# P V of an attention block in 64x64 tiles by blocks of 64 keys, in two stages over two PSUM banks

## The chip, the cores and the metric

One core of one Trainium2 chip. The metric is the device time of one execution in microseconds. TensorE is PE in the profile (its weight loads PEld), VectorE DVE, ScalarE ACT, GpSimd POOL, SyncE SP.

## The reference

Eight sequences of 256 tokens, model width 128. Each is normalised and goes through causal attention with 16 heads of 64 and, beside it, through a feed-forward block with ternary weights (width 512); both are added to the input.

```python
xn = _layernorm(x, axis=-1)
# attention, on a second normalisation of xn with weight ln_w and bias ln_b
q, k, v = (einsum('bsd,hde->bshe', x2, W) + bias for each)
scores  = einsum('bqhe,bkhe->bhqk', q, k) * 64 ** -0.5     # -inf where key > query
pattern = softmax(scores, axis=-1)
z       = einsum('bhqk,bkhe->bqhe', pattern, v)             # the "P V" of the title
attn    = einsum('bqhe,hed->bqd', z, W_o) + b_o
h       = relu(einsum('bsd,fd->bsf', xn, ternary(W1)) + b1)
ffn     = einsum('bsf,df->bsd', h, ternary(W2)) + b2
out     = x + attn + ffn
```

## The kernel before

The host lays each sequence out "by place": tokens 0 to 127, then 192 to 255, then 128 to 191. So places 128 to 191 hold the last 64 tokens. A "pair" is two heads (8 pairs), a "duo" is two pairs (4 duos). Batch is one sequence.

For each batch the steps are: normalisation (POOL, with statistics on DVE); its transposes xh and xn on PE; eight projections pr0 to pr7 (queries and keys of one pair, three f32r passes of high and low parts) with a copy to qk on ACT (L474, L476); four value products v0 to v3 (half of the heads by half of the tokens) with a copy to v on DVE (L622); scores s0 to s7 per pair, plain f32 in 64x64 tiles of PE (L816): row half by head, column half by query block; per head maxima m on DVE (L597) and exponentials e on ACT (L485, L487); reciprocals i on DVE; division p on POOL (L308, L309); a 32x32-block transpose t on DVE per pair (L610); then d, four transfers per duo issued by SP (L345) that bring the blocks into pT; then z, the product of v and the turned probabilities per duo (`heads`, L834 to L860); its high part zT_hi on ACT (L497) and its low part zT_lo on DVE (L616); f0, f1 and h0, h1, the feed-forward; and the output product in two parts, oa and ob, closed on DVE by o and stored by SP (st).

In `heads`, per pair and head, the keys of token tile 0 (128 partitions, all rows of PE) are multiplied for all 256 queries, and the keys of tile 1 for the 128 later queries only; the two heads of a pair stand in the two column halves of PE. So there are 8 matmuls per duo, in f32, and each matmul is two records in the profile. All of them go into one PSUM bank of 512 f32: pair 0 in its first half, pair 1 in its second.

The order of work on every engine is written out by hand in strings: a head (batches 0 and 1), a plan that is repeated for batches 2 to 6, and a tail (batch 7). Each engine works through its own string in order. In a string, `s3` is scores of pair 3, `z1-` is heads of duo 1 of the batch before, `pr0+` a projection of the next batch. On PE the number behind the colon is the PSUM bank (of four in m_ps) into which the step writes; before it writes, `wait_taken` (L732) waits until the step that had this bank before was read out. Scores have banks of their own (s_ps, two pairs by two heads), so scores of pair n wait for the exponentials of pair n - 2 (L811). For the bank of heads the step that sets it free is zT_lo on DVE.

In the last batch the last two pairs are not turned by DVE and transfers but by PE (tw, tn), since nothing is left to hide the transfers.

## Time and profile before

| | us |
|---|---|
| median of 3 runs | 227.62 (227.01 to 228.51) |
| profiled execution | 227.57 |
| its span, first to last instruction | 225.8 |
| PE busy in the span | 216.5 (96%) |
| DVE busy | 201.5 (89%) |
| ACT busy | 195.4 (87%) |
| POOL busy | 184.8 (82%) |

The granted clock was 1.00 in all stretches, that is 2.4 GHz. The span is smaller than the device time by what lies around the first and the last instruction. In the timeline and in the chain a row gives start and length; matmuls overlap, so what a block costs PE is the distance from its start to the next block's start and not its length. A fused row ("x40") stands for so many records of the same line.

### The profile page before, as it was taken

The numbers are of one execution on the slowest core, as the hardware profiler recorded it, in microseconds if no ns is written. First come the engines' busy times: TensorE is split into PE (matmuls) and PEld (weight loads), VectorE is DVE, ScalarE is ACT, GpSimd is POOL, SyncE is SP. The second block draws the span as 40 slices with busy tenths as digits, with TensorE's granted clock in tenths as the row PEclk, the third lists the DMA queues.
The fourth block names the chain that finished last, engine by engine and source line by source line (L and its number), as shares of the span: only waits on it lengthen the run. The fifth ranks groups of instructions, "written<-read, shape, count | busy, mean of one in ns | idle before, by whom it ended". The sixth has DMA issues, their size and how long they took to land.

```text
span 225.8 us, 7611 instructions
## 1 busy us (share of the span) xinstructions
PE 216.5 (96%) x2646; PEld 182.9 (81%) x2646; DVE 201.5 (89%) x776; ACT 195.4 (87%) x733; POOL 184.8 (82%) x363
## 2 busy tenths in 40 slices
...
GB/s 155 300 247 3 116 167 141 140 66 126 142 139 142 119 117 137 154 104 149 165 142 142 104 131 133 144 103 142 172 127 169 73 137 134 180 105 192 207 41 23
DMA packets 24022, 30.66 MB, mean 136 GB/s; under 512 B 2608, under 2 KB 23088, under 8 KB 23984
## 3 DMA queue, kind: packets, MB, share of 16 engines
...
q14 instruction: 17, 0.14, 0.2%
...
## 4 chain that ended last, share of the span: by engine, by line
PE 41%; POOL 20%; ACT 15%; DVE 12%; DMA 6%; issue 2%; SPq 2%; POOLq 0%; DVEq 0%
PE s_ps L816 8%; PE m_ps L854 7%; POOL prob L309 5%; ACT prob L485 5%; DMA pT<-blocks 4%; POOL prob L308 4%; ACT prob L487 4%; DVE s_ps L597 4%; PE m_ps L781 4%; DVE blocks L610 4%; POOL xn_cur L388 3%; PE m_ps L858 3%; PE m_ps L782 3%; PE m_ps L783 3%; ACT qk L474 2%
## 5 line engine op out<-in xcount | busy, mean ns | idle before, releaser
L485 ACT ACTIVATE prob<-s_ps,neg_max 128x256 f32<-128x256 f32 x128 | 69.3, 541 | 10.5 <-DVE neg_max L597 10.3
L597 DVE CUSTOM_DVE_ANT_0 s_ps<-s_ps,causal 128x256 f32<-128x256 f32 x128 | 54.7, 427 | 8.3 <-PE s_ps L816 8.1
L309 POOL TENSOR_SCALAR prob<-prob,inv_sum 128x256 f32<-128x256 f32 x126 | 61.6, 489 | 0.0
L610 DVE STREAM_TRANSPOSE blocks<-prob 128x768 f32<-128x768 f32 x62 | 58.8, 962 | 0.8 <-POOL prob L309 0.3
L308 POOL TENSOR_SCALAR prob<-prob,inv_sum 128x128 f32<-128x128 f32 x126 | 48.1, 382 | 13.4 <-DVE inv_sum L604 13.3
L487 ACT ACTIVATE prob<-s_ps,neg_max 128x128 f32<-128x128 f32 x128 | 55.4, 433 | 0.0
L816 PE MATMUL s_ps<-qk 64*64 64x64 f32 (+2 forms) x1280 | 46.7, 278 | 0.8 <-ACT prob L487 0.7
L816 PEld LDWEIGHTS s_ps<-qk 64*64 64x64 f32 x1280 | 39.1, 132 | 9.7 <-issue 4.7
L854 PE MATMUL m_ps<-pT,v 128*64 128x256 f32 x256 | 40.0, 388 | 2.5 <-DMA pT<-blocks 2.5
L597 DVE CUSTOM_DVE_ANT_0 s_ps<-s_ps,causal_first 128x128 f32<-128x128 f32 x128 | 42.3, 331 | 0.0
L474 ACT ACTIVATE qk<-m_ps,vecs 128x256 f32<-128x256 f32 x64 | 34.9, 546 | 2.0 <-PE m_ps L783 1.6
L597 DVE DVE_READ_ACCUMULATOR2_ANT neg_max<- 128x1 f32 x256 | 36.1, 141 | 0.0
L476 ACT ACTIVATE qk<-m_ps,vecs 128x256 f32<-128x256 f32 x64 | 35.3, 553 | 0.0
L487 ACT ACTIVATION_READ_ACCUMULATOR prob<-s_ps,neg_max 128x1 f32 x128 | 34.6, 270 | 0.0
L485 ACT ACTIVATION_READ_ACCUMULATOR prob<-s_ps,neg_max 128x1 f32 x128 | 33.7, 263 | 0.0
L858 PEld LDWEIGHTS m_ps<-pT,v 128*64 128x64 f32 x256 | 19.1, 137 | 8.5
L858 PE MATMUL m_ps<-pT,v 128*64 128x128 f32 x256 | 25.2, 273 | 0.0
L616 DVE TENSOR_TENSOR zT_lo<-m_ps,zT_hi 128x512 fp32r<-128x512 f32 x32 | 21.9, 686 | 2.7 <-ACT zT_hi L497 2.4
L497 ACT ACTIVATE zT_hi<-m_ps 128x512 fp32r<-128x512 f32 x32 | 20.7, 647 | 3.6 <-PE m_ps L858 3.5
L622 DVE COPY v<-m_ps 128x512 f32<-128x512 f32 x32 | 21.6, 678 | 0.3 <-PE m_ps L804 0.3
L439 POOL TENSOR_TENSOR hT_lo<-hT,hT_hi 128x512 fp32r<-128x512 f32 x16 | 20.7, 1291 | 1.3
L854 PEld LDWEIGHTS m_ps<-pT,v 128*64 128x64 f32 x256 | 15.1, 136 | 5.4 <-issue 3.3
...
## 6 DMA issues: line engine op xcount, KB each, us to landing
...
```

Of the source, the lines that this page charges most:

```text
L308: op(first, first, inv_sum[:, j, 2 + h:3 + h], 0.0, ALU.mult, ALU.add)
L309: last = op(later, later, inv_sum[:, j, h:h + 1], 0.0, ALU.mult, ALU.add)
L474: nc.scalar.activation(qk[:, j, 0, :], halves("pr", pair, b)[:, 0, :], ACT.Identity, bias=vecs[:, BQ + pair:BQ + pair + 1])
L476: last = nc.scalar.activation(qk[:, j, 1, :].rearrange("e (g j k) -> e g j k", g=TILES, j=QT), halves("pr", pair, b)[:, 1, :].rearrange("e ...
L485: nc.scalar.activation(later, s_ps[:, pair % 2, h, 0:S].rearrange("p (g j k) -> p g j k", g=TILES, j=QT), ACT.Exp, bias=neg_max[:, j, h:h ...
L487: nc.scalar.activation(first, s_ps[:, pair % 2, h, S:W].rearrange("p (j k) -> p j k", j=QT), ACT.Exp, bias=neg_max[:, j, 2 + h:3 + h], sca ...
L597: last = nc.vector.tensor_tensor_reduce(out=sc, in0=sc, in1=mask, scale=-SCALE, scalar=-MASKED, op0=ALU.add, op1=ALU.min, accum_out=neg_ma ...
L610: nc.vector.transpose(blocks[:, duo, :, n, :, :], prob[:, pair % NBUF, :, :, :, :] .rearrange("p h j g k -> p (j g) h k")).then_inc(turned, 1)
L616: nc.vector.tensor_tensor(zT_lo[:, both, :], halves("z", duo, b), zT_hi[:, both, :].bitcast(F32), ALU.subtract).then_inc(z_lo, 1)
L816: return nc.tensor.matmul(at[side * E:side * E + E], qk[rows, j, 0, places], keys[rows], start=True, stop=True)
L854: nc.tensor.matmul(dst[h * E:h * E + E, n, :], v[:, 0, cols], turned_parts(n, h)[0], start=True, stop=False)
L858: last = nc.tensor.matmul(dst[h * E:h * E + E, n, P:S], v[:, 1, cols], turned_parts(n, h)[1], start=False, stop=True)
```

## The change

Heads are worked in 64x64 tiles. The keys of a token tile are split into two blocks of 64, one in each row half of PE, and every product is cut to the queries that may see the block: keys 0 to 63 by all 256 queries, keys 64 to 127 by 192 of them, keys 128 to 191 by 128, keys 192 to 255 by 64. `heads(b, duo, stage)` has two stages. In stage 0 (step y) the first row half works on the duo's pair 0 and the later row half on pair 1, in stage 1 (step z) the row halves work on the other pair. Pair 0 is accumulated in one PSUM bank and pair 1 in another, so that a step x (which issues nothing) and the step y each name a bank; the two row halves never write into one bank within a stage. Stage 1 waits for stage 0 by a new semaphore, heads_half. Stage 0 has 5 products, stage 1 has 7, each for two heads: 24 matmuls per duo instead of 8. The copies of heads on ACT and DVE read 256 columns from each of two banks instead of 512 of one.

The orders of all engines are new, also in the head and the tail. In the steady plan y and z of duos 0 to 3 of the batch before now stand among the first part of the batch, with a block of scores between y and z of each duo.

The diff, cut; head and tail strings are left out here but for PE's tail and the first line of ACT's head, the two of the new text that stand between.

```diff
--- before
+++ after
...
-PE_PLAN = ("z1-:2 s1 pr4:3 v0:0 pr5:2 v1:1 pr6:3 s2 s3 oa-:2 f0:3 z2-:1 z3-:0 s4 s5 pr7:1 v2:3 ob- v3:3 xh+:0 "
-           "f1:2 s6 s7 z0:0 pr0+:1 pr1+:2 pr2+:3 pr3+:1 xn+:0 s0+")
...
-ACT_PLAN = ("pr7- e9- e10- e11- xh f1- e12- e13- z0- pr0 e14- pr1 e15- xn pr2 e0 z1- e1 pr3 pr4 e2 e3 pr5 pr6 e4 "
-            "e5 e6 e7 z2- z3- f0 e8")
...
-DVE_PLAN = ("m1 xn z1- m2 t7- m3 v0 ln+ i0 i1 m4 v1 m5 t0 i2 m6 m7 t1 t2 z2- m8 z3- m9 m10 i3 v2 m11 o- i4 t3 xh+ "
-            "m12 m13 v3 m14 i5 i6 m15 z0 t4 t5 m0+ i7 t6")
...
-POOL_PLAN = ("p0 p1 p2 ln+ p3 xl+ p4 p5 p6 p7 h0 h1")
...
-SP_PLAN = ("d1- d2- d3- d0 st-")
...
+PE_PLAN = ("s0 x0-:1 y0-:2 s1 z0- pr4:0 pr5:3 x1-:1 y1-:2 s2 z1- v0:0 pr6:3 x2-:2 y2-:1 s3 z2- s4 pr7:3 v1:0 "
+           "x3-:2 y3-:1 s5 z3- s6 v2:3 v3:0 xh+:2 oa-:1 f0:0 f1:2 s7 pr0+:0 xn+:3 pr1+:2 ob- pr2+:0 pr3+:3")
+PE_TAIL = ("s0 x0-:0 y0-:1 s1 pr4:2 z0- x1-:3 s2 y1-:2 z1- x2-:0 y2-:1 s3 z2- pr5:2 v0:3 s4 pr6:2 v1:3 pr7:0 "
+           "x3-:2 y3-:1 s5 z3- s6 oa-:3 ob- x0:0 y0:1 s7 z0 v2:2 f0:3 x1:0 y1:1 z1 tw6:2 v3:3 x2:1 tw7:0 tn3:2 "
+           "f1:3 y2:0 z2 x3:3 y3:2 z3 oa:1 ob oc")
+ACT_HEAD = ("wh0 wh1 pr0 wh2 xn pr1 wh3 e0 e1 pr2 aa e2 pr3 e3 pr4 pr5 e4 e5 pr6 pr7 f0 e6 e7 xh+ e8 e9 xn+ f1 "
...
+ACT_PLAN = ("e13- e14- pr0 xn e15- pr1 pr2 pr3 e0 z0- e1 e2 pr4 pr5 z1- e3 e4 e5 pr6 z2- e6 e7 e8 e9 pr7 z3- e10 "
+            "xh+ e11 e12 f0 f1")
...
+DVE_PLAN = ("ln+ m2 z0- m3 i0 t7- m4 m5 z1- t0 i1 v0 m6 m7 z2- m8 m9 t1 i2 v1 m10 m11 i3 z3- v2 m12 i4 v3 xh+ t2 "
+            "t3 i5 m13 m14 m15 i6 t4 t5 xn+ t6 o- i7 m0+ m1+")
...
+POOL_PLAN = ("p1 ln+ p2 p3 xl+ p4 p5 p6 h0 p7 p0+ h1")
...
+SP_PLAN = ("d3- d0 d1 d2 st-")
...
+        def heads_banks(duo, b):
+
+            low, high = sorted((BANK["x", duo, b], BANK["y", duo, b]))
+            return m_ps[:, low:high + 1:high - low, 0:S]
...
-                wait(sp, z_psd, DUOS * (b - 1) + duo + 1)
+                wait(sp, z_psd, 4 * (DUOS * (b - 1) + duo + 1))
...
-                wait(act, z_psd, PAIRS // 2 * b + duo + 1)
-                nc.scalar.activation(zT_hi[:, 2 * duo:2 * duo + 2, :], halves("z", duo, b), ACT.Copy).then_inc(z_hi, 1)
+                wait(act, z_psd, 4 * (DUOS * b + duo + 1))
+                nc.scalar.activation(zT_hi[:, 2 * duo:2 * duo + 2, :], heads_banks(duo, b), ACT.Copy).then_inc(z_hi, 1)
...
-                nc.vector.tensor_tensor(zT_lo[:, both, :], halves("z", duo, b), zT_hi[:, both, :].bitcast(F32),
+                nc.vector.tensor_tensor(zT_lo[:, both, :], heads_banks(duo, b), zT_hi[:, both, :].bitcast(F32),
...
-                elif kind == "z":
+                elif kind in "xy":
...
-            def heads(b, duo):
-                if duo % 2 == 0:
-                    wait(pe, v_done, 4 * b + duo + 2)
+            def heads(b, duo, stage):
                 by_tensor = on_tensor_engine(b, 2 * duo)
-                if by_tensor:
-                    pe.wait_ge(last_wide, 2)
-                    pe.wait_ge(last_narrow, 1)
+                dst = heads_banks(duo, b)
+                first, later = slice(0, E), slice(E, P)
+                whole, lower, upper, near, far, both = (slice(0, QT), slice(0, 2), slice(2, QT), slice(0, 1), slice(1, 2),
+                                                        slice(0, 2))
+                def product(n, rows, tile, queries, i, done=None, closes=False):
+                    clears = tile == 0 and rows == (first if n == 0 else later) and queries.start == 0
+                    toks = slice(queries.start * P + i.start * QB, (queries.stop - 1) * P + i.stop * QB)
+                    for h in range(2):
+                        cols = slice((2 * (2 * duo + n) + h) * E, (2 * (2 * duo + n) + h) * E + E)
+                        if by_tensor:
+                            turned_part = pT_last[rows, n, h, tile * P + toks.start:tile * P + toks.stop]
+                        else:
+                            turned_part = pT[rows, duo, i, tile + queries.start:tile + queries.stop, n, h, :]\
+                                .rearrange("p i g q -> p g i q")
+                        last = nc.tensor.matmul(dst[h * E:h * E + E, n, toks], v[rows, tile, cols], turned_part,
+                                                start=clears, stop=closes)
+                        if done is not None:
+                            last.then_inc(done, 1)
+                if stage == 0:
+                    if duo % 2 == 0:
+                        wait(pe, v_done, 4 * b + duo + 2)
+                    if by_tensor:
+                        pe.wait_ge(last_wide, 2)
+                        pe.wait_ge(last_narrow, 1)
+                    else:
+                        pe.wait_ge(pT_in[duo], 16 * QT * (b + 1))
+                    product(0, first, 0, both, whole)
+                    product(1, later, 0, near, upper)
+                    product(1, later, 0, far, whole)
+                    product(1, later, 1, far, whole, heads_half)
+                    product(0, first, 1, far, lower, heads_half)
                 else:
-                    pe.wait_ge(pT_in[duo], 16 * QT * (b + 1))
-                dst = halves("z", duo, b)
-
-                def turned_parts(n, h):
-                    if by_tensor:
-                        return pT_last[:, n, h, 0:S], pT_last[:, n, h, S:W]
-                    return pT[:, duo, :, 0:2, n, h, :].rearrange("p i g q -> p g i q"), pT[:, duo, :, 2, n, h, :]
-
-                for n in range(2):
-                    pair = 2 * duo + n
-                    for h in range(2):
-                        cols = slice((2 * pair + h) * E, (2 * pair + h) * E + E)
-                        nc.tensor.matmul(dst[h * E:h * E + E, n, :], v[:, 0, cols], turned_parts(n, h)[0],
-                                         start=True, stop=False)
-                    for h in range(2):
-                        cols = slice((2 * pair + h) * E, (2 * pair + h) * E + E)
-                        last = nc.tensor.matmul(dst[h * E:h * E + E, n, P:S], v[:, 1, cols], turned_parts(n, h)[1],
-                                                start=False, stop=True)
-                last.then_inc(z_psd, 1)
+                    wait(pe, heads_half, 4 * (DUOS * b + duo + 1))
+                    product(0, later, 0, near, upper)
+                    product(1, first, 0, near, lower)
+                    product(0, later, 0, far, whole)
+                    product(1, first, 0, near, upper)
+                    product(1, first, 0, far, whole)
+                    product(0, later, 1, far, whole, z_psd, closes=True)
+                    product(1, first, 1, far, lower, z_psd, closes=True)
...
+                elif kind == "x":
+                    pass
+                elif kind == "y":
+                    heads(b, index, 0)
                 elif kind == "z":
-                    heads(b, index)
+                    heads(b, index, 1)
```

## Rows read from the trace of the kernel before

**Rows 1.** The page, part 1: busy time, share of span, and instructions of each engine.

```profile
PE 216.5 (96%) x2646; PEld 182.9 (81%) x2646; DVE 201.5 (89%) x776; ACT 195.4 (87%) x733; POOL 184.8 (82%) x363
```

**Rows 2.** Stretches: from and to, length, busy time of each engine, clock, DMA share, GB/s.

```profile
12.00:39.00 27.00, 25.66 (x293) 19.96 (x295) 25.22 (x107) 26.72 (x105) 25.38 (x46) 1.00 0.54 130
...
64.60:89.80 25.20, 25.20 (x332) 21.93 (x328) 23.89 (x93) 23.00 (x91) 20.42 (x43) 1.00 0.60 133
89.80:115.60 25.80, 25.57 (x334) 22.09 (x328) 24.69 (x99) 23.63 (x92) 22.36 (x46) 1.00 0.60 137
115.60:141.90 26.30, 25.32 (x334) 22.11 (x329) 24.70 (x96) 23.80 (x92) 22.85 (x46) 1.00 0.60 135
141.90:167.20 25.30, 25.30 (x333) 22.01 (x329) 23.92 (x93) 23.10 (x90) 21.01 (x42) 1.00 0.55 132
...
190.40:210.00 19.60, 19.31 (x258) 15.98 (x253) 18.66 (x75) 18.63 (x74) 16.78 (x35) 1.00 0.71 158
```

**Rows 3.** Waits from 64 to 167 us: waiter, releaser, us in total, times, longest.

```profile
PE m_ps L854 <- DMA pT<-blocks: 1.2, 2, 1.0
...
DVE s_ps L597 <- PE s_ps L816: 3.5, 11, 0.6
...
ACT prob L485 <- DVE neg_max L597: 7.0, 14, 0.9
```

**Rows 4.** Timeline of PE, 98 to 104 us: start, length, line, operation.

```profile
98.08 0.65 PE L854 MATMUL m_ps<-pT,v 128*64 128x256 f32 x4
...
100.52 0.39 PE L858 MATMUL m_ps<-pT,v 128*64 128x128 f32 x4
100.84 1.34 PE L816 MATMUL s_ps<-qk 64*64 64x256 f32 x40
102.10 0.38 PE L781 MATMUL m_ps<-x2T_hi,wq_lo 128*128 128x256 f32 x1
...
102.92 0.40 PE L802 MATMUL m_ps<-wv_hi,x2T_lo 128*128 128x512 f32 x1
...
103.62 0.28 PE L924 MATMUL m_ps<-zT_hi,wo_lo 128*128 128x256 f32 x1
```

**Rows 5.** Timeline of PE, 113 to 116 us.

```profile
113.45 0.65 PE L854 MATMUL m_ps<-pT,v 128*64 128x256 f32 x4 [0.22 <-DMA pT<-blocks]
...
114.90 0.78 PE L816 MATMUL s_ps<-qk 64*64 64x256 f32 x20
115.61 0.39 PE L781 MATMUL m_ps<-x2T_hi,wq_lo 128*128 128x256 f32 x1
```

**Rows 6.** Chain that ended last, 131 to 140 us: start, length, what.

```profile
131.59 0.99 DVE blocks L610
132.60 0.55 SPq L345
...
134.58 5.00 DMA pT<-blocks
...
139.72 0.65 PE m_ps L854 x4
```

**Rows 7.** Groups by line, shapes apart: busy us and mean ns, then idle before.

```profile
L616 DVE TENSOR_TENSOR zT_lo<-m_ps,zT_hi 128x512 fp32r<-128x512 f32 x32 | 21.9, 686 | 2.7 <-ACT zT_hi L497 2.4
...
L497 ACT ACTIVATE zT_hi<-m_ps 128x512 fp32r<-128x512 f32 x32 | 20.7, 647 | 3.6 <-PE m_ps L858 3.5
```

**Rows 8.** Timeline of ACT, 88 to 90 us.

```profile
88.10 0.56 ACT L474 ACTIVATE qk<-m_ps,vecs 128x256 f32<-128x256 f32 x1
...
88.82 0.58 ACT L485 ACTIVATE prob<-s_ps,neg_max 128x256 f32<-128x256 f32 x1
...
89.61 0.72 ACT L497 ACTIVATE zT_hi<-m_ps 128x512 fp32r<-128x512 f32 x1
90.11 0.59 ACT L485 ACTIVATE prob<-s_ps,neg_max 128x256 f32<-128x256 f32 x1
```

**Rows 9.** Timeline of DVE, 91 to 93 us.

```profile
90.97 0.42 DVE L597 CUSTOM_DVE_ANT_0 s_ps<-s_ps,causal 128x256 f32<-128x256 f32 x1
...
91.56 0.97 DVE L610 STREAM_TRANSPOSE blocks<-prob 128x768 f32<-128x768 f32 x1
92.45 0.40 DVE L597 CUSTOM_DVE_ANT_0 s_ps<-s_ps,causal 128x256 f32<-128x256 f32 x1
```

More of the change, by code:

```diff
@@ L48 @@
 BUSY = (5, 1)
-PE_HEAD = ("xb:0 pr0:0 pr1:3 xn:2 s0 s1 v0:3 pr2:1 pr3:2 v1:3 s2 v2:1 s3 pr4:3 ta:0 pr5:2 pr6:1 s4 pr7:3 v3:0 "
-           "xh+:1 f0:2 s5 s6 pr0+:0 bo:2 f1:1 pr1+:3 s7 xn+:0 z0:1 s0+ pr2+:3 pr3+:2 pr4+:0 s1+ pr5+:1 z1:3 s2+ "
-           "z2:2 s3+ pr6+:0 oa:3 f0+:1 s4+ z3:0 s5+ v0+:1 v1+:2 pr7+:0 ob v2+:1 v3+:2 xh++:3 f1+:0 s6+ s7+ z0+:1 "
-           "pr0++:0 pr1++:2 pr2++:3 xn++:0 pr3++:1 s0++")
-PE_PLAN = ("z1-:2 s1 pr4:3 v0:0 pr5:2 v1:1 pr6:3 s2 s3 oa-:2 f0:3 z2-:1 z3-:0 s4 s5 pr7:1 v2:3 ob- v3:3 xh+:0 "
-           "f1:2 s6 s7 z0:0 pr0+:1 pr1+:2 pr2+:3 pr3+:1 xn+:0 s0+")
@@ L55 @@
-PE_TAIL = ("pr4:2 s1 z1-:3 v0:0 s2 pr5:1 pr6:0 s3 z2-:2 s4 pr7:3 s5 z3-:1 oa-:0 f0:3 s6 s7 f1:1 v1:3 v2:2 v3:1 "
-           "ob- z0:3 z1:2 tw6:1 tn3:0 tw7:3 z2:1 z3:0 oa:2 ob oc")
-ACT_HEAD = ("wh0 wh1 pr0 pr1 wh2 wh3 xn e0 e1 pr2 e2 e3 pr3 aa e4 e5 pr4 e6 e7 pr5 pr6 e8 xh+ e9 f0 pr7 e10 e11 "
-            "pr0+ e12 f1 e13 pr1+ e14 z0 xn+ e15 pr2+ oh e0+ e1+ pr3+ e2+ e3+ pr4+ z1 wh4 e4+ pr5+ e5+ e6+ pr6+ "
-            "z2 e7+ f0+ wh5 z3 e8+")
-ACT_PLAN = ("pr7- e9- e10- e11- xh f1- e12- e13- z0- pr0 e14- pr1 e15- xn pr2 e0 z1- e1 pr3 pr4 e2 e3 pr5 pr6 e4 "
-            "e5 e6 e7 z2- z3- f0 e8")
@@ L62 @@
-ACT_TAIL = ("pr7- e9- e10- e11- xh f1- e12- e13- z0- pr0 e14- pr1 e15- pr2 xn e0 pr3 e1 z1- pr4 e2 e3 e4 e5 pr5 "
-            "e6 e7 pr6 pr7 e8 z2- e9 z3- e10 e11 f0 f1 e12 e13 e14 e15 z0 w6 w7 z1 z2 z3")
-DVE_HEAD = ("lz nh xb wl0 wl1 m0 m1 xn v0 m2 i0 m3 ln+ v1 i1 t0 m4 m5 m6 v2 th i2 m7 te0 m8 m9 i3 t1 v3 xh+ m10 "
[3 rows of a table removed]
-DVE_PLAN = ("m1 xn z1- m2 t7- m3 v0 ln+ i0 i1 m4 v1 m5 t0 i2 m6 m7 t1 t2 z2- m8 z3- m9 m10 i3 v2 m11 o- i4 t3 xh+ "
-            "m12 m13 v3 m14 i5 i6 m15 z0 t4 t5 m0+ i7 t6")
-DVE_TAIL = ("m1 xn m2 t7- m3 i0 v0 m4 m5 z1- m6 i1 m7 i2 t0 m8 t1 m9 i3 m10 t2 m11 i4 t3 z2- i5 z3- t4 m12 t5 m13 "
-            "m14 v1 i6 m15 v2 v3 i7 o- q7 z0 n3 z1 z2 z3 o")
@@ L72 @@
-POOL_HEAD = ("hs np wl2 wl3 p0 ln+ p1 p2 p3 xl+ p4 h0 p5 h1 p6 p7 ol p0+ p1+ wl4 ln++ wl5 p2+ p3+ h0+ xl++ p4+ p5+ "
-             "p6+ p7+ h1+")
-POOL_PLAN = ("p0 p1 p2 ln+ p3 xl+ p4 p5 p6 p7 h0 h1")
-POOL_TAIL = ("p0 p1 p2 p3 p4 p5 h0 h1 p6")
-SP_HEAD = ("d0 d1 d2 d3 d0+ st")
-SP_PLAN = ("d1- d2- d3- d0 st-")
-SP_TAIL = ("d1- d2- d3- d0 d1 d2 st- st")
+PE_HEAD = ("xb:2 pr0:0 pr1:3 xn:2 s0 v0:1 pr2:3 s1 v1:1 pr3:3 s2 pr4:1 ta:0 pr5:2 s3 pr6:3 f0:0 pr7:2 s4 v2:3 "
[3 rows of a table added]
+PE_PLAN = ("s0 x0-:1 y0-:2 s1 z0- pr4:0 pr5:3 x1-:1 y1-:2 s2 z1- v0:0 pr6:3 x2-:2 y2-:1 s3 z2- s4 pr7:3 v1:0 "
+           "x3-:2 y3-:1 s5 z3- s6 v2:3 v3:0 xh+:2 oa-:1 f0:0 f1:2 s7 pr0+:0 xn+:3 pr1+:2 ob- pr2+:0 pr3+:3")
```

13 lines of the change are left out of this document (added), and 9 rows, old and new, of tables (DVE_HEAD, PE_HEAD).

## The prediction, made before the change was run

> **What bounds the kernel now.** I read the busy shares first: PE, DVE, ACT and POOL lie between 216.5 and 184.8 us of a 225.8 us span [rows 1], so the share alone does not name the bound. The table of stretches does. Its cuts are where the fifth pair of projections of batches 2, 3, 4, 5 and 6 begins: four batches in 25.2, 25.8, 26.3 and 25.3 us, mean 25.65, with PE busy all the time in two of them, and DVE on average (23.89 + 24.69 + 24.70 + 23.92) / 4 = 24.3 us, ACT 23.4, POOL 21.7 [rows 2]. The waits of the same stretch say it again: PE waited 1.2 us in 103, for two late loads of pT; DVE waited 3.5 us for PE's scores, and ACT 7.0 us for DVE's maxima [rows 3]. So in the steady part PE's order sets the time, 0.3 us per batch is lost to transfers, and DVE is the next bound, only 1.3 us per batch below. In the first part (12 to 39 us) ACT is busy 26.72 of 27.00 us, and in 190 to 210 us ACT 18.63 of 19.60 [rows 2]: there a shorter PE gives little.
>
> **PE, the part that is removed.** Start to start, four heads halves in a row (two duos of 16 records) run from 98.08 to 100.84: 1.38 us a duo; one alone between scores runs from 113.45 to 114.90: 1.45 us [rows 4, 5]. The old steady plan has z2 z3 together and z1 and z0 alone: 2.76 + 2 x 1.45 = 5.66 us per batch. Scores: alone 0.71 us (114.90 to 115.61), two in a run 1.26 (100.84 to 102.10), so one more block in an unbroken run of 64x64 tiles costs 0.55 and each run pays 0.16 for entering and leaving [rows 4, 5]. Old scores: two alone, three runs of two: 2 x 0.71 + 3 x 1.26 = 5.20. Together 10.86 us.
>
> **PE, the part that is added.** A pair of heads streams 256 + 128 columns through all rows. In blocks of 64 keys a row half streams 256 + 64 for one pair, and 64 + 128 + 128 for the other, so 320 columns in each stage, the two halves side by side, the two heads in the column halves. That is what a scores block does: per column half 256 + 64 and 128 + 64 + 128, ten products, twenty records, and two banks. The first stage also has ten products. I therefore price it at 0.55. The second stage has fourteen products for the same 320 columns; no row shows it. Below: 0.55, as its columns are the same. Above: 0.71, a block that pays for a run of its own [rows 5]. I take 0.60, since it is nearest to the scores block. The new plan has five runs of 64x64 work per batch (s0 y0 s1 z0; y1 s2 z1; y2 s3 z2 s4; y3 s5 z3 s6; s7), 16 blocks: 5 x 0.71 + 11 x 0.55 + 4 x 0.05 = 9.80 us. PE gains 10.86 - 9.80 = 1.06 per batch, 1.26 with the lower bound and 0.62 with the upper. The wait of the second stage for the first costs nothing in this plan: a block of scores (0.55) lies between. Where y and z stand side by side (two places in the head, three in the tail) the drain is on PE; below 0, above 0.39, the length of the last records of a heads block [rows 4]. These at most 2.0 us lie mostly where ACT leads, and at the very end the cheaper blocks pay them back (two duos 2.76 before, 4 x 0.58 + 2 x 0.2 = 2.7 after), so I book nothing.
>
> By the Trainium skill (TensorE: Matmul & The Clock Gate, Part 3, the mechanism of packing) matmuls start and end strictly in program order, also across tiles. Then a tile would stand still while another works off its turn. Counted through for a scores block, with two passes to a product and each pass begun only after the one before has begun, that is 448 column times where the tiles side by side need 320. The trace disagrees: at 0.55 / 320 = 1.72 ns a column the rule would give 0.77 us, and a further block takes 0.55 [rows 4, 5].
>
> **ACT, DVE and POOL** do the same work. The copy of the heads (647 ns) and its low part (686 ns) [rows 7] now read 256 columns from each of two banks instead of 512 from one; same count of elements, so nothing is added. Eight semaphore increments per duo instead of one are sent by matmuls that are there anyway. I cost both at 0 and at most 0.1 per duo, on the chain only where the next paragraph says.
>
> **What becomes late.** PE without waits would need 25.65 - 0.3 - 1.06 = 24.3 us, the same as DVE's busy time. So PE can gain 1.35 per batch at the very most, and new waits take from it. I went through a batch from s0 at 0 with durations of rows: scores of 0.55, a projection after scores 0.82 (102.10 to 102.92), values 0.70 (102.92 to 103.62) [rows 4], maxima 0.59 a head, a turn 0.89 [rows 9], exponentials 0.79, a pair of projections on ACT 0.72, heads 0.50 [rows 8].
> First, banks. The old plan gave the heads one of four banks, the new one gives them two (1 and 2), from y to the end of the low part. z0 ends near 2.2, is in PSUM near 2.45; 0.65 on ACT and 0.69 on DVE behind what stands ahead of them give 4.0. PE wants y1 after pr4 and pr5 at 3.95. z1 is in PSUM at 5.95; ACT has pr4 and pr5 ahead until 6.05, then 0.65 and 0.69: 7.45; PE wants y2 at 7.4. So both are met with about 0.1 us each, no more.
> Second, transfers. t7 of the batch before stands on DVE behind statistics, a maximum, z0, a maximum: it ends near 5.4. In the trace a turn that ended at 132.58 let its heads start at 139.72: issue of four transfers on SP, then 5.00 us for the last one, 7.1 us in all [rows 6]. PE wants y3 (after y2 s3 z2 s4 pr7 v1) at 11.4; the data is there at 5.4 + 7.1 = 12.5 at the latest. The other pT wait of the trace was 0.2 long, so the way is often shorter; with 6.4 it is 11.8. The wait is 0.4 to 1.1; behind it in PE's queue stand s5, z3, s6, and DVE and ACT wait for those scores. In the old plan z3 came after oa and f0, at 98.08 + 1.38 = 99.46, 6.9 behind the end of t7 at 92.53 [rows 4, 9]. I take 0.5. s6 also needs the exponentials e8 and e9, which ACT ends near 13.5, about when PE comes there, so this wait is covered by the one before it.
> Sum: 24.3 + 0.1 (banks) + 0.5 (pT) = 24.9, 0.75 less than 25.65. The steady part is 39 to 190 us, six batches; the first and last have ACT's load near them, so I count five and a bit: 5.3 x 0.75 = 4.0 us. The profiled execution took 227.57 us, 0.05 below the median of 227.62, so both give **223.6 us**.
>
> **Rivals.**
> A, waits come to nothing: y3 finds its data, the banks turn in time. DVE bounds, 24.4: 5.3 x 1.25 = 6.6, **221 us**. For it: ACT and DVE still have 2.2 and 1.3 us of slack per batch [rows 2]. Against: 7.1 us from turn to heads is a measured row.
> B, the saving is eaten: y3 waits its full 1.1 (24.3 + 0.1 + 1.1 = 25.5, 0.15 x 5.3 = 0.8 us less), or the second stage costs 0.71 (0.44 more per batch) and the wait is 0.7: about **227 us**. For it: DVE and PE would both be full, with two score buffers between them, so that a wait of one is soon a wait of the other.
> C, slower: the transfer of the last duo sets the period. It is a loop: t7, 7.1 us, y3, s5, maxima, and on to the next t7. If t7 ends later than 5.4, because DVE waits there for ACT's copy of z0, each 0.1 us goes onto the batch. The gain is gone when that wait is 25.65 - 24.3 - 0.1 = 1.25, with 7.1 us of way that is t7's end at 11.4 + 1.25 - 7.1 = 5.55; it costs more than 1% (2.3 / 5.3 = 0.43 a batch) from 6.0 on. With t7 at 6.2 the wait is 1.9 and the batch 26.3: 0.65 x 5.3 = 3.4, **231 us**. Against it: 7.1 is the longest case of the trace, not the usual one.
> D, the row halves don't run side by side, so that products go in turn (the rule named above): the first stage is 448 column times, 0.77, the second 384, 0.66, together 1.43 a duo, nothing gained over 1.38 to 1.45 but fewer changes of tile, and the new waits stay: 25.65 - 0.3 + 0.1 + 0.5 = 25.95, **229 us**. Against it: [rows 4, 5], where four tiles of scores do run side by side.
>
> **Chances.** Forecast (222.3 to 225.2) 0.43; A 0.15; B 0.26; C 0.12; D 0.04. The predicted time is the forecast's. The range goes from 220.0, A's lower part, to 229.5, which leaves out most of C. A difference under about 1% can't be told from none here. Faster by over 1% (below 225.3): forecast and A, 0.58. Within 1%: B and half of D, 0.28. Slower: C and the other half, 0.14.
>
> **What would show it.** Steady batches of about 24.9 us instead of 25.65; blocks of the first stage 0.55 and of the second 0.55 to 0.71 apart in a run; DVE busy about 24.3 per batch, as before; a wait of PE for pT of 0.5 once per batch ahead of y3, with pT the first name in PE's waits; small waits of PE for DVE's zT_lo. ACT's waits for DVE's maxima should shrink. The prediction falls if the second stage is above 0.71, if DVE's or ACT's heads instructions grow by reading two banks, or if PE's waits exceed 1.4 us per batch.

## The result

The changed kernel takes 226.56 us (median of 20 runs, 225.15 to 228.59), the kernel before 227.8 us (20 runs, 227.01 to 229.64): ratio 0.9926, 95% interval 0.9902 to 0.9949. The ratio compares means, 226.41 against 228.10, and leaves out one slow run of the changed kernel (228.59). It is 0.7% faster, where 1.8% was forecast; the range held, the sign was right, the size was not. The profiled execution took 226.65 us, 0.92 less than that of before.

The page of the changed kernel, part 1, and its stretches, cut again where the fifth pair of projections of a batch begins (from 62.60 on: batches 2 to 6):

```profile
PE 212.5 (95%) x3670; PEld 187.4 (83%) x3670; DVE 202.1 (90%) x776; ACT 195.7 (87%) x733; POOL 182.5 (81%) x363
```

```profile
62.60:87.60 25.00, 24.41 (x461) 22.55 (x456) 24.27 (x97) 23.27 (x91) 22.85 (x45) 1.00 0.64 145
87.60:113.30 25.70, 24.80 (x463) 22.66 (x457) 24.66 (x97) 23.55 (x92) 21.93 (x44) 1.00 0.59 134
113.30:138.30 25.00, 24.19 (x460) 22.33 (x456) 24.39 (x96) 23.39 (x92) 21.86 (x44) 1.00 0.61 140
138.30:163.30 25.00, 24.66 (x463) 22.68 (x457) 24.37 (x97) 23.34 (x92) 21.84 (x44) 1.00 0.60 140
```

Against [rows 1] PE has 1,024 records more and 4 us less busy time. DVE, ACT and POOL have the same number of instructions and the same load within 1.3%. Against [rows 2] a batch is shorter, but PE is no longer busy all the time in any of them. The waits from 64 to 167 us, PE first, then its weight loads:

```profile
PE m_ps L863 <- DMA pT<-blocks: 1.9, 3, 0.8
PE s_ps L823 <- ACT prob L494: 0.2, 1, 0.2
```

```profile
PEld m_ps L863 <- issue: 3.7, 5, 1.2
PEld m_ps L863 <- DVE zT_lo L623: 1.7, 7, 0.3
```

The wait for pT (1.9 against 1.2 in [rows 3]) is larger and stands ahead of one step, y3. The wait for zT_lo is new: it is the PSUM banks of the heads. "Issue" stands on the same line, ahead of weight loads of the heads.

PE's timeline for most of a batch, from s0 to v2 (starts of blocks are what counts):

```profile
110.90 0.78 PE L823 MATMUL s_ps<-qk 64*64 64x256 f32 x20
111.50 0.74 PE L863 MATMUL m_ps<-pT,v 64*64 64x256 f32 x20
112.05 0.75 PE L823 MATMUL s_ps<-qk 64*64 64x256 f32 x20
112.60 0.75 PE L863 MATMUL m_ps<-pT,v 64*64 64x64 f32 x28
113.28 0.38 PE L788 MATMUL m_ps<-x2T_hi,wq_lo 128*128 128x256 f32 x1
...
115.04 0.78 PE L863 MATMUL m_ps<-pT,v 64*64 64x256 f32 x20
...
118.51 0.79 PE L863 MATMUL m_ps<-pT,v 64*64 64x256 f32 x20
119.08 0.77 PE L823 MATMUL s_ps<-qk 64*64 64x256 f32 x20
119.62 0.78 PE L863 MATMUL m_ps<-pT,v 64*64 64x64 f32 x28
120.24 0.78 PE L823 MATMUL s_ps<-qk 64*64 64x256 f32 x20
120.96 0.38 PE L788 MATMUL m_ps<-x2T_hi,wq_lo 128*128 128x256 f32 x1
121.76 0.39 PE L809 MATMUL m_ps<-wv_hi,x2T_lo 128*128 128x512 f32 x1
...
123.31 0.78 PE L863 MATMUL m_ps<-pT,v 64*64 64x256 f32 x20 [0.70 <-DMA pT<-blocks]
123.88 0.77 PE L823 MATMUL s_ps<-qk 64*64 64x256 f32 x20
124.43 0.78 PE L863 MATMUL m_ps<-pT,v 64*64 64x64 f32 x28
125.00 0.76 PE L823 MATMUL s_ps<-qk 64*64 64x256 f32 x20
125.69 0.50 PE L809 MATMUL m_ps<-wv_hi,x2T_lo 128*128 128x512 f32 x1
```

Stage 0 takes 0.55 to 0.57 (111.50 to 112.05, 118.51 to 119.08), stage 1 takes 0.57 to 0.62 ahead of scores (124.43 to 125.00, 119.62 to 120.24) and 0.68 ahead of a projection (112.60 to 113.28). From s0 at 110.90, y1 starts at +4.14, y2 at +7.61, y3 at +12.41; the walk of the prediction had 4.0, 7.5 and 11.8 to 12.5. Values v1 at 121.76 should let y3 start 0.8 later; it starts 1.55 later.

### The profile page after: what moved, and what is told of

Same layout as the page of the kernel before. It is cut to its first block, busy times and chain, and to the rows that moved or that the text cites. A ratio compares the mean times of both kernels' runs of the same rounds, so it can differ in the third digit from the quotient of the medians.

```text
span 224.9 us, 9676 instructions
## 1 busy us (share of the span) xinstructions
PE 212.5 (95%) x3670; PEld 187.4 (83%) x3670; DVE 202.1 (90%) x776; ACT 195.7 (87%) x733; POOL 182.5 (81%) x363
## 3 DMA queue, kind: packets, MB, share of 16 engines
HBM read 4.73 MB, written 1.05 MB: 26 GB/s over the span
## 4 chain that ended last, share of the span: by engine, by line
PE 38%; DVE 23%; DMA 11%; ACT 10%; POOL 8%; SPq 4%; issue 3%; POOLq 0%; DVEq 0%
DMA pT<-blocks 11%; DVE s_ps L604 9%; PE m_ps L863 6%; PE s_ps L823 6%; DVE blocks L617 6%; SPq L352 4%; ACT prob L492 3%; PE m_ps L941 3%; ACT prob L494 2%; PE m_ps L788 2%; PE s_ps L734 2%; DVE neg_max L604 2%; PE m_ps L790 2%; PE m_ps L789 2%; DVE zT_lo L623 2%
## 5 line engine op out<-in xcount | busy, mean ns | idle before, releaser
L492 ACT ACTIVATE prob<-s_ps,neg_max 128x256 f32<-128x256 f32 x128 | 65.4, 511 | 2.6 <-DVE neg_max L604 2.3
L863 PE MATMUL m_ps<-pT,v 64*64 64x64 f32 (+2 forms) x1536 | 50.0, 257 | 5.9 <-DMA pT<-blocks 3.5
L863 PEld LDWEIGHTS m_ps<-pT,v 64*64 64x64 f32 x1536 | 42.8, 133 | 12.1 <-issue 5.8
L494 ACT ACTIVATE prob<-s_ps,neg_max 128x128 f32<-128x128 f32 x128 | 51.7, 404 | 0.0
L823 PE MATMUL s_ps<-qk 64*64 64x128 f32 (+2 forms) x1280 | 49.7, 275 | 0.8 <-ACT prob L494 0.6
L823 PEld LDWEIGHTS s_ps<-qk 64*64 64x64 f32 x1280 | 42.1, 133 | 5.6 <-issue 3.3
L481 ACT ACTIVATE qk<-m_ps,vecs 128x256 f32<-128x256 f32 x64 | 33.8, 528 | 1.1 <-PE m_ps L784 0.8
L483 ACT ACTIVATE qk<-m_ps,vecs 128x256 f32<-128x256 f32 x64 | 34.3, 536 | 0.0
L494 ACT ACTIVATION_READ_ACCUMULATOR prob<-s_ps,neg_max 128x1 f32 x128 | 31.0, 242 | 0.0
L492 ACT ACTIVATION_READ_ACCUMULATOR prob<-s_ps,neg_max 128x1 f32 x128 | 30.2, 236 | 0.0
L788 PE MATMUL m_ps<-x2T_hi,wq_lo 128*128 128x256 f32 x56 | 18.7, 333 | 0.8 <-issue 0.6
L510 ACT ACTIVATE hT<-m_ps,vecs 128x256 f32<-128x256 f32 x32 | 12.8, 478 | 3.4 <-PE m_ps L930 3.4
```

The source lines that it names most:

```text
L481: nc.scalar.activation(qk[:, j, 0, :], halves("pr", pair, b)[:, 0, :], ACT.Identity, bias=vecs[:, BQ + pair:BQ + pair + 1])
L483: last = nc.scalar.activation(qk[:, j, 1, :].rearrange("e (g j k) -> e g j k", g=TILES, j=QT), halves("pr", pair, b)[:, 1, :].rearrange("e ...
L492: nc.scalar.activation(later, s_ps[:, pair % 2, h, 0:S].rearrange("p (g j k) -> p g j k", g=TILES, j=QT), ACT.Exp, bias=neg_max[:, j, h:h ...
L494: nc.scalar.activation(first, s_ps[:, pair % 2, h, S:W].rearrange("p (j k) -> p j k", j=QT), ACT.Exp, bias=neg_max[:, j, 2 + h:3 + h], sca ...
L788: nc.tensor.matmul(dst, wlo[kind][:, cols], x2T_hi[:, :], start=True, stop=False)
L823: return nc.tensor.matmul(at[side * E:side * E + E], qk[rows, j, 0, places], keys[rows], start=True, stop=True)
```

## Where the time of a steady batch went

The distance from each PE block's start to the next one's, for the five batches between s0 of batch 2 and s0 of batch 7, splits a batch. The least distance that a block shows in any batch of the kernel and of its variants with equal blocks (three executions of the kernel before, seven of the changed one) is taken as its cost without a wait; what is above it is counted as waiting. The split leans on this choice: with each kernel's own execution alone the waits are 0.73 and 1.10, and the blocks save 0.86. The length of a batch comes from one profiled execution of each kernel; differences of a tenth between two runs mean little.

| us per batch | before | changed | difference | predicted |
|---|---|---|---|---|
| s0 to s0 of the next batch, mean of five | 25.73 | 25.24 | -0.48 | -0.75 |
| sum of the blocks without waits | 24.88 | 23.83 | -1.05 | -1.06 |
| waits | 0.84 | 1.41 | +0.57 | +0.3 |

In the kernel before, 0.39 of the waits stand ahead of z1; the rest is in pieces below 0.08. In the changed kernel they are ahead of y3 (0.68), of y1 (0.18, banks), and after z1 and z3 (0.10 each); the rest is in pieces below 0.06.

The saving of the blocks hides two errors that cancel: the sixteen blocks of heads and scores went from 10.88 to 9.61 (forecast: 10.86 to 9.80), but the other blocks went from 14.00 to 14.21. The new order has five runs of heads and scores a batch instead of four, and a projection or values block behind a 64x64 run or ahead of one takes 0.77 to 0.80 from start to start, where one between two of its like takes 0.68 to 0.69. Of this the prediction had only what the scores blocks show.

From s0 of batch 2 to s0 of batch 7 the changed kernel wins 2.4 us (before: 61.10 to 189.72; changed: 60.22 to 186.43). At s0 of batch 2 it is 0.88 ahead, but has still to do a duo of heads (y0 and z0, 1.23 us) that the old order had behind it: like for like it is 0.35 late. From s0 of batch 7 to the end it takes 2.4 us longer, of which 1.23 are that duo: 1.1 to 1.2 us are lost in the tail. 2.4 - 0.35 - 1.15 = 0.9, the difference of the two spans.

## The experiments

Ratios are to runs of the kernel before on the same chip, with their 95% intervals; they can differ by up to 0.2% from the quotient of the two medians. The changed kernel's own is 0.993 (0.990 to 0.995).

**1. Old products in the new order.** What do the tiles give, what does the order?

```diff
             def heads(b, duo, stage):
+                if stage == 0:
+                    return
...
+                        nc.tensor.matmul(dst[h * E:h * E + E, n, :], v[:, 0, cols], turned_parts(n, h)[0],
+                                         start=True, stop=False)
...
+                last.then_inc(z_psd, 4)
```

> The new orders, banks and copies, but the old heads: step y issues nothing, step z issues the eight matmuls over all rows, each pair into its own bank. Theory (the products save PE about 1.1 us per batch in this order; the new waits for banks and pT eat half of it, the tail the rest): steady batches grow from 25.2 to 25.9-26.4 us, the total to 230-233 us, ratio to before 1.01 to 1.025. Rival (the orders carry the 0.7% gain, the tiles nothing): the total stays at 226-227 us.

Measured: 231.39 us, ratio 1.0153 (1.0123 to 1.0183). The orders carry nothing by themselves: with the old products they cost 1.5%, and the tiles turn that into a gain of 0.7%, 2.3% between the two. A steady batch takes 25.99 us (61.17 to 191.14 for five) against 25.24 and 25.73. In 64 to 167 us PE has no wait of 0.2 us or more for pT: with dearer heads PE reaches z3 after its transfer has landed. So the products save 0.75 a batch in this order. The five batches of this run agree block by block within 0.02 us, and their blocks add up to 25.98 against 23.83: the products take up to 2.15 off PE's blocks here (less by whatever wait stands alike in every batch of this run), and most of it comes back as waits. What the new products would do in the old order was not run.

**2. The wait ahead of y3 taken away.** The heads of duo 3 read duo 2's part of pT.

```diff
-                        pe.wait_ge(pT_in[duo], 16 * QT * (b + 1))
+                        pe.wait_ge(pT_in[2 if duo == 3 else duo], 16 * QT * (b + 1))
...
-                            turned_part = pT[rows, duo, i,
+                            turned_part = pT[rows, 2 if duo == 3 else duo, i,
```

> The changed kernel, but in batches 0 to 6 the heads of duo 3 read the turned probabilities of duo 2, whose transfers have landed long before (all transfers are still made; wrong values for duo 3's heads). It takes away the wait ahead of y3 alone. Theory (this wait costs 0.5 us a batch and is on PE's path): PE's waits for pT in 64 to 167 us fall from 1.9 to near 0, steady batches 24.7 us, total 224-225 us. Rival (DVE or the banks would hold PE at the same place anyway): steady batches stay at 25.1-25.2, total within 0.5 us of the changed kernel.

Measured: 224.81 us, ratio 0.9865 (0.9838 to 0.9893); a steady batch is 25.02. The wait of 0.68 is gone, but only 0.22 of it is won. PE's timeline around y3 in this run:

```profile
120.98 0.39 PE L809 MATMUL m_ps<-wv_hi,x2T_lo 128*128 128x512 f32 x1
...
121.77 0.78 PE L863 MATMUL m_ps<-pT,v 64*64 64x256 f32 x20
122.36 0.74 PE L823 MATMUL s_ps<-qk 64*64 64x256 f32 x20
122.91 0.81 PE L863 MATMUL m_ps<-pT,v 64*64 64x64 f32 x28
123.92 0.78 PE L823 MATMUL s_ps<-qk 64*64 64x256 f32 x20 [0.20 <-ACT prob L494]
```

y3 comes 0.79 after v1, without a wait. But from z3 to s6 it is now 1.01 instead of 0.57 (124.43 to 125.00 above): s6 waits for the exponentials of pair 4. That wait was named in the prediction as "covered by the one before it". Over the five batches 0.26 of the 0.68 stand there now, 0.15 between y3 and s5 (in one batch), and 0.11 around z1.

**3. The banks released early.** ACT and DVE read a quarter of each heads bank, release it, and spend the other three quarters on SBUF.

```diff
-                nc.scalar.activation(zT_hi[:, 2 * duo:2 * duo + 2, :], heads_banks(duo, b), ACT.Copy).then_inc(z_hi, 1)
+                nc.scalar.activation(zT_hi[:, 2 * duo:2 * duo + 2, 0:E], heads_banks(duo, b)[:, :, 0:E], ACT.Copy).then_inc(z_hi, 1)
+                nc.scalar.activation(zT_hi[:, 2 * duo:2 * duo + 2, E:S],
+                                     wo[:, 0:3, :].rearrange("p a d -> p (a d)").rearrange("p (n s) -> p n s", n=2), ACT.Copy).then_inc(z_rest, 1)
...
+                nc.vector.tensor_tensor(zT_lo[:, both, 0:E], heads_banks(duo, b)[:, :, 0:E], zT_hi[:, both, 0:E].bitcast(F32),
+                                        ALU.subtract).then_inc(z_free, 1)
+                still = wo[:, 0:3, :].rearrange("p a d -> p (a d)").rearrange("p (n s) -> p n s", n=2)
+                nc.vector.tensor_tensor(zT_lo[:, both, E:S], still, still, ALU.subtract).then_inc(z_lo, 1)
```

> The changed kernel, but the two PSUM banks of a duo come free after a quarter of the heads copies: ACT and DVE read 64 of 256 columns of each bank, then release it, and spend the rest of the time on 384 columns read from SBUF (three quarters of the heads values are replaced, so the output is another). Turn-round of a bank shrinks by about 0.8 us, the load of ACT and DVE grows by about 0.1 to 0.3 us a duo for the second instruction. Theory (waiting for banks costs 0.4 us a batch): PE's waits for zT_lo go to 0, steady batches 24.8-25.0 us, total 224-226 us. Rival (DVE bounds the steady part): steady batches longer, 25.3 or more, by the added DVE time.

Measured: 230.53 us, ratio 1.0113 (1.007 to 1.0155). Both halves of the expectation came: no wait of PE for zT_lo is left in 64 to 167 us, and the batches got longer, 25.52. The stretch 65 to 165 us, first of the changed kernel, then of this one:

```profile
65.00:165.00 100.00, 97.41 (x1813) 89.54 (x1802) 96.99 (x376) 92.85 (x358) 87.52 (x176) 1.00 0.61 140
```

```profile
65.00:165.00 100.00, 97.39 (x1760) 88.75 (x1762) 97.39 (x385) 93.06 (x371) 88.72 (x173) 1.00 0.60 137
```

The added instructions cost DVE 4.7 us over the run (206.8 busy against 202.1) and ACT 2.8; POOL is busy 6.9 us longer with no instruction of its own added. The span grows by 3.8 us: 1.6 up to s0 of batch 2, 1.4 in five steady batches, 0.8 behind them. What the banks alone cost is not told by it, nor which of the three engines costs the time.

**4. DVE relieved, in both kernels.** Each copy of values moves half of its columns from batch 1 on.

```diff
-                nc.vector.tensor_copy(v[:, t, HALF[half]], bank("v", n, b)).then_inc(v_done, 1)
+                copied = H * E // 4 if b else H * E // 2
+                nc.vector.tensor_copy(v[:, t, half * H * E // 2:half * H * E // 2 + copied], bank("v", n, b)[:, 0:copied]).then_inc(v_done, 1)
```

> The changed kernel with DVE relieved: from the second batch on each of the four copies of values moves 256 of 512 columns (the other half of v keeps the first batch's values), about 0.27 us less each, 1.1 us of DVE per batch. Theory (after the change PE is still the first bound, with waits for pT and banks, and DVE second): steady batches 25.2 to 24.9 us, total 0.5 to 1.5 us less than the changed kernel. Rival (DVE bounds the steady part now): batches 24.2 to 24.4 us, total 4 to 5 us less, 222 us.

> The same relief of DVE in the kernel before. Theory (PE sets the time there, waiting 1.2 us in 103): steady batches fall by 0.2 us or less from 25.7, total by up to 1 us. Rival (DVE is already part of the bound): total 3 us less or more.

Measured: changed kernel 225.48 us, 0.9907 (0.987 to 0.9945); before 227.42 us, 0.9996 (0.9958 to 1.0034). Steady batches 25.17 and 25.68, each 0.05 to 0.07 less for 0.8 us less DVE work (23.7 instead of 24.5 busy in a batch; the expectation had 1.1). The sum of DVE's work bounds neither, and the rival falls; the theory's 24.9 did not come either. The copies of values lie outside the stretch of DVE that experiment 5 finds in the chain.

**5. PE relieved, in both kernels.** The output product leaves out the low part of the hidden values.

```diff
-                for hid in (hT_hi, hT_lo):
+                for hid in (hT_hi,):
```

> The changed kernel with PE relieved: the output product leaves out the four matmuls on the low part of the hidden values, about 0.57 us of PE per batch (the output loses that low part); they stand behind z3 and ahead of f0, so f0, f1 and s7 come earlier. Theory (PE's path with its waits still sets the time): steady batches 25.2 to 24.7 us, total 2 to 3 us less than the changed kernel. Rival (DVE bounds, or the waits fill what PE gives): 1 us less or nothing.

> The same relief of PE in the kernel before. Theory (PE sets the time): steady batches 25.7 to 25.15 us, total 2.5 to 3 us less than before. Rival (the other engines hold it): 1 us less. Against the run with the same relief of the changed kernel it tells how much of a PE saving each order passes on.

Measured: changed kernel 224.65 us, 0.9875 (0.9829 to 0.9921); before 227.16 us, 0.9973 (0.9941 to 1.0006). Here the theory fell. The steady batch is 25.17 in the changed kernel (0.07 less) and 25.86 in the kernel before (0.13 more), for 0.45 us less PE work in each batch. Over eight batches 3.6 us of work are gone, and by the ratios the kernel before wins 0.3% of its time (0.6% at most, 1.4 us) and the changed one 0.5%; most of what the changed kernel wins, it wins in the tail (s0 of batch 7 comes 0.3 earlier, s7 0.8, the end 1.6). The waits of PE for pT, of before with less PE work, and of the changed kernel with less PE work:

```profile
PE m_ps L854 <- DMA pT<-blocks: 3.0, 5, 1.1
PEld m_ps L854 <- issue: 4.0, 6, 1.3
```

```profile
PE m_ps L863 <- DMA pT<-blocks: 3.2, 3, 1.4
```

1.2 in [rows 3] became 3.0, and 1.9 became 3.2. So a second bound lies as close as PE's own work, in the kernel before already: a chain that goes round once per batch. Two rows of DVE in the changed kernel show its first part, from s0 (at 110.90) to t7:

```profile
111.77 0.43 DVE L604 CUSTOM_DVE_ANT_0 s_ps<-s_ps,causal 128x256 f32<-128x256 f32 x1 [0.49 <-PE s_ps L823]
...
115.53 0.95 DVE L617 STREAM_TRANSPOSE blocks<-prob 128x768 f32<-128x768 f32 x1
```

DVE waits for s0 (0.5 to 0.6 us in four of five batches) and then works without a pause until t7, which starts 4.63 after s0 in all five steady batches of the changed kernel and of its variant with less PE work, however early PE comes. Then come the transfer, 6.1 to 7.6 us from t7's end to y3, and PE's steps from y3 to the next s0: in the mean 5.58 + 6.80 + 12.87 us, the batch of 25.24. In the kernel before it is s0, t7 (4.5 to 5.2 behind it), transfer, z3, PE's steps from z3 to s0.

Where the relief lies in this chain differs. In the kernel before, oa stands between s0 and z3, beside the transfer and not in the chain: of its 0.48 nothing is won, and z3, which never waited, now starts 0.58 later behind z2. In the changed kernel oa stands behind y3, in the chain, and its 0.48 should count. They do not: 0.22 more stand ahead of y3, where the transfers of this execution took 0.16 longer on average (6.96 instead of 6.80), and 0.27 stand around pr3, whose bank DVE frees with the low part of xn:

```profile
109.21 0.39 DVE L680 TENSOR_TENSOR xnT_lo<-m_ps,xnT_hi 128x256 fp32r<-128x256 f32 x1
```

```profile
109.65 0.19 PEld L788 LDWEIGHTS m_ps<-x2T_hi,wq_lo 128*128 128x128 f32 x1
```

So the chain through the transfer alone does not tell what a saving is worth. By these rows PE's order, the chain and DVE's order lie within about half a microsecond of each other. Both engines relieved at once was not run.

**6. Both waits at once, and the wait of the kernel before.** Experiment 2 with experiment 5; and the kernel before with duo 1 reading duo 0's part of pT.

```diff
+                    source = 0 if duo == 1 and b < B - 1 else duo
-                    pe.wait_ge(pT_in[duo], 16 * QT * (b + 1))
+                    pe.wait_ge(pT_in[source], 16 * QT * (b + 1))
```

> Both at once in the changed kernel: heads of duo 3 of batches 0 to 6 read duo 2's turned probabilities (no wait ahead of y3), and the output product leaves out the four matmuls on the low part of the hidden values (0.57 us of PE a batch). With the wait in place the second alone moved the steady batch by 0.07 us. Theory (the transfer loop hid PE's saving; without it PE sets the time): steady batches fall from 25.0 to 24.5 us. Rival (DVE, busy 24.4 us a batch, or the banks hold it): 24.9 or more.

> The kernel before, but in batches 0 to 6 the heads of duo 1 read the turned probabilities of duo 0 (transfers are still made, duo 1's values are wrong). It takes away the wait ahead of z1. Theory (the kernel before already stands on the edge of such a loop, with a wait of 0.2 to 1.0 us in some batches): steady batches 25.7 to 25.3 us, total 1.5 to 2 us less. Rival (those waits only happened in the profiled execution): no change.

Measured: 223.46 us, 0.9825 (0.9777 to 0.9873), batch 24.84; and 227.7 us, 1.0006 (0.9978 to 1.0033), batch 25.81. Without the transfer's wait PE's saving passes on a little more (25.02 to 24.84, 0.18 of 0.45, between the theory's 24.5 and the rival's 24.9): s6's wait for exponentials, the banks and pr2, pr3 take the rest. In the kernel before, the expectation fell (and so did its rival, since the waits moved): the wait ahead of z1 is gone and stands ahead of the heads of duo 3 instead. Its timeline:

```profile
98.79 0.60 PE L855 MATMUL m_ps<-pT,v 128*64 128x256 f32 x4
...
100.22 0.65 PE L855 MATMUL m_ps<-pT,v 128*64 128x256 f32 x4 [0.61 <-DMA pT<-blocks]
```

The second of the two duos starts at 100.22, 2.13 behind the first at 98.09; in [rows 4] both took 2.76 without a wait, 1.38 each. So in the kernel before the transfers of duo 1 and of duo 3 both land about when PE comes for them, and taking one wait away uncovers the other.

**7. The turn of pair 7 earlier.** A change that leaves nothing out.

```diff
-DVE_PLAN = ("ln+ m2 z0- m3 i0 t7- m4 m5 z1-
+DVE_PLAN = ("ln+ m2 z0- t7- m3 i0 m4 m5 z1-
...
-            "o- t5 m14 m15 z0 i6
+            "t5 o- m14 m15 z0 i6
```

> The changed kernel with two places of DVE's order exchanged: in the steady plan t7 directly after z0 of the batch before, ahead of m3 and i0 (0.65 to 0.7 us earlier), and in the tail t5 ahead of the output o (0.4 us earlier). Nothing is left out. Theory (a loop holds the steady part: t7, transfer of duo 3, y3 s5 z3 ... s0 y0 s1 z0, copies of z0, t7): PE's wait ahead of y3 goes, steady batches 25.2 to 25.0 us as in the run without that wait, the tail 0.3 us less, total 1 to 1.5 us less than the changed kernel, 225.3, ratio 0.987. Rival (m3 and the exponentials behind it then hold s3): no gain or 0.5 us more.

Measured: 226.81 us, ratio 0.9969 (0.9948 to 0.999). PE's waits for pT in 64 to 167 us:

```profile
PE m_ps L863 <- DMA pT<-blocks: 0.3, 1, 0.3
```

1.9 became 0.3: the transfer is in time. The batch stays at 25.23. The blocks show where it went: ahead of y3 0.14 instead of 0.68, but z3 to s6 0.29 instead of 0.10, 0.13 more ahead of y0, 0.18 around pr3 and 0.06 ahead of y2. On DVE m3 comes 0.9 later (t7 now stands ahead of it); that the moved waits hang on it is argued. The rival held.

**8. Stages apart.** y and z of a duo not next to each other in three places.

```diff
-            "f1:3 y2:0 z2 x3:3 y3:2 z3 oa:1 ob oc")
+            "f1:3 y2:0 x3:3 y3:2 z2 z3 oa:1 ob oc")
...
-  x0:2 s7 y0:1 z0 s0+     and     x3:3 y3:2 z3 s5+
+  x0:2 s7 y0:1 s0+ z0     and     x3:3 y3:2 s5+ z3
```

> The changed kernel with three pairs of steps moved in PE's order so that z does not follow its y: in the tail y2 y3 z2 z3 instead of y2 z2 y3 z3, in the head s0+ before z0 and s5+ before z3. Everything else the same. Theory (a y directly followed by its z costs 0.91 to 0.96 us instead of 0.55, and the two at the end are on the chain): y2 to the output product 2.3 instead of 3.27 us, total 0.7 to 1.0 us less than the changed kernel, 225.6. Rival (the end is set by the transfer of duo 2 and by the copies of z2 and z3): 0.3 us or less.

Measured: 228.48 us, ratio 1.001 (0.9976 to 1.0043), slower than the changed kernel; neither theory had that. In the head it loses 1.3 us up to s7 of batch 1, 0.7 of them ahead of s4 (s4 45.03 became 45.74, s7 54.74 became 56.02, and s0 of batch 2 from 60.22 to 61.51). At the end:

```profile
216.41 0.78 PE L863 MATMUL m_ps<-pT,v 64*64 64x256 f32 x20
217.41 1.90 PE L863 MATMUL m_ps<-pT,v 64*64 64x256 f32 x76 [0.21 <-ACT hT L510]
220.28 0.74 PE L941 MATMUL m_ps<-hT_hi,w2T 128*128 128x256 f32 x4 [0.97 <-DVE zT_lo L623]
```

y2 to oa is 3.87 us instead of 3.27. The last blocks are closer together, but y3 waits 0.21 for f1's copy to leave its bank, and oa waits 0.97 for the bank of y2, which comes free only after z2 and both copies of its heads. With all four banks under two duos, the place of z2 helps to decide when oa can begin.

**9. The last scores earlier.** Only the tail's order.

```diff
-  s6 oa-:3 ob- x0:0 y0:1 s7 z0 v2:2
+  s6 oa-:3 s7 ob- x0:0 y0:1 z0 v2:2
...
-            "o- t5 m14 m15 z0 i6 v2 i7 q7 z1 v3 n3 z2 z3 o")
+            "t5 m14 m15 o- i6 z0 v2 i7 q7 z1 v3 n3 z2 z3 o")
```

> The changed kernel with another order in the tail alone, nothing left out: on PE the last scores s7 come ahead of ob of batch 6, y0 and z0 (by 1.4 + 0.55 us of PE work earlier), on DVE the output o of batch 6 moves from ahead of t5 to behind the last maxima, and values v2 and the low heads go between the last reciprocals as their inputs come. Rival 1 (the tail gives 2.4 us back because s7 stands behind work that the old tail had behind it, and a fixed chain of maxima, exponentials, division, transposes and four heads blocks follows s7): y2 of batch 7 starts 1.5 to 2 us after less time from s0 of batch 7, the total falls by 1.5 us to 225.0. Rival 2 (DVE is full from 197 to 206 us, and t5 with its transfer, and the last maxima, wait for DVE and not for PE): only the 0.4 us of o are won, total 0.5 us less or no difference that can be measured.

Measured: 227.07 us, ratio 0.9965 (0.9939 to 0.999). s7 starts at 204.50 instead of 206.38, y2 at 215.15 instead of 214.93. Rival 1 fell: 1.9 us at s7 are worth nothing at the end. Rival 2's half microsecond did not come either. The trace shows why. The turn of pair 5, moved ahead of o, waits 0.26 for POOL's division and starts at 206.40 instead of 206.55. And y2 no longer waits for its transfer but for the steps ahead of it, of which tw7 needs the bank of z1: the low part of z1 ends at 213.58, tw7 starts at 213.68, y2 at 215.15.

## Why the prediction was right or wrong

**PE's blocks: right.** Predicted 0.55 and 0.60 for the stages, 9.80 us for heads and scores, 1.06 saved; measured 0.55 to 0.57 and 0.57 to 0.62, 9.61 for heads and scores, and 1.05 on the sum of all blocks, since the others became 0.2 dearer, which the prediction did not have. That the second stage's four more products cost nearly nothing more is a row now. Row halves run side by side, so rival D (and the rule of the Trainium skill, TensorE: Matmul & The Clock Gate, Part 3, that matmuls start and end strictly in program order also across tiles) is out for these matmuls: as the prediction counts it through, it would have asked 0.66 us for stage 1 and 0.77 for stage 0.

**"PE's order sets the time" as the first reading: wrong as put, and this is the step that failed.** The prediction took PE's 1.2 us of waits in 103 [rows 3] for all of its slack, 0.3 a batch, and let a saving on PE come through but for 0.3 of new waits. The blocks show up to 0.84 of waits a batch in the kernel before, and experiment 5 shows that 0.45 us less PE work there buys nothing in a steady batch. The chain from s0 through t7 and its transfer back to s0 is as long as PE's own work. The prediction has this loop, in rival C, but only as a danger if t7 came late; it did not come late (it ends 5.58 behind s0, forecast 5.4), and the loop held the batch all the same.

In numbers: of the forecast 4.0 us, 0.9 came (by the two profiled executions). In steady batches 0.48 each was won instead of 0.75, and five of them count, not 5.3: 2.4 instead of 4.0. The other 1.5 are lost in head and tail, below. The measured time lies near rival B's 227, but neither of B's two conditions held (y3's wait was 0.68 and not 1.1, the second stage 0.62 at most and not 0.71), so B was not right by its mechanism; only its remark that a wait of one engine is soon a wait of another fits.

**The new waits: named rightly, sized too low.** Forecast: 0.5 for y3, 0.1 for the banks, 24.9 for the batch. Measured: 0.68 for y3, about 0.2 for the banks at y1 and y2, and 0.5 more behind z1, z3 and in small pieces elsewhere: 1.41 in all on a floor of 23.83, just past the 1.4 at which the prediction said it would fall. The floor was forecast 0.5 too high (24.3) and the waits 0.8 too low (0.6), and 25.24 came of it. The time of y3's data (+11.8 to +12.5 after s0) was right: +12.41. Waits moved instead of going away: taking y3's wait away (experiment 2) or moving its data forward (experiment 7) made s6 wait for exponentials.

**Head and tail: the second failed term.** I took 5.3 batches' gain for the whole gain and booked nothing for y next to z. Five batches won 2.4 us and only 0.9 reached the end. A y that its z follows at once costs 0.91 to 0.96 from start to start instead of 0.55, in six places (I had counted five): 0.36 to 0.41 each, 2.3 us of PE. Four of them lie in the tail, and 4 x 0.38 = 1.5 is more than the 1.15 us lost there; "the cheaper blocks pay them back" was wrong at the end, where y2 to oa takes 3.27 us and z2 to oa took 2.75:

```profile
206.63 0.90 DVE blocks L617
207.55 0.54 SPq L352
...
209.50 5.30 DMA pT<-blocks
...
214.93 0.92 PE m_ps L863 x13
215.90 1.47 PE m_ps L863 x38
217.41 0.80 PE m_ps L863 x24
218.20 1.19 PE m_ps L941 x8
```

This is the chain that ended last: the turn of pair 5, its transfer (7.4 us from turn to heads, like [rows 6]), then y2, z2 with y3, z3. That these four steps are 0.5 dearer at the end is shown by the starts. That the other 0.6 us of the tail come from y next to z is argued, not shown: experiments 8 and 9 changed the tail's order and found the banks and the copies between z and the next y in the way instead. Two things hold y2 at 215 us: in the changed kernel it waits 0.37 for its transfer, and with the last scores earlier the steps ahead of it, tied to the banks of z1, end no sooner (experiment 9).

**Heads copies over two banks: right.** 684 ns on DVE and 617 on ACT against 686 and 647 in [rows 7]. **DVE as the next bound: not reached by its sum of work.** It is busy 24.4 of 25.2 us, and 0.8 us less of it moves a batch by 0.07. But its 4.6 us from s0 to t7 are a part of the chain, and with less PE work PE waits for it at pr3.

No version beat the changed kernel without leaving work out: experiments 7 to 9 are within or behind it.
